# Adding the target rows by an accumulating gather instead of on VectorE, in a graph network's first edge pass

## What is computed

```python
s_n, v_n = _equiv_layernorm(s, v, gamma_s, beta_s, gamma_v)
msg_s = (s_n @ Ws_src)[src] + (s_n @ Ws_dst)[dst]
msg_v = einsum(v_n, Wv_src)[src] + einsum(v_n, Wv_dst)[dst]
w1 = rbf @ W_rbf
m1_s, m1_v = _cg_tp(msg_s, msg_v, y0, y1, w1[...])     # products of msg with the edge's y and w1
a = leaky_relu(m1_s @ W_alpha) . alpha_dot             # logits of a softmax over the edges of a target
val_s, val_v = m1_s @ Ws_val, einsum(m1_v, Wv_val)     # gated, then a second product and h per edge
agg = segment_sum(softmax(a) * h, dst)
```

## Time and profile before

| | before |
|---|---|
| median of 3 runs | 8057.24 us |
| lowest to highest run | 8041.64 to 8085.88 us |
| span of the profiled execution | 8045.0 us |
| VectorE busy, whole span | 7086.7 us, 88% |
| PE busy, whole span | 6926.1 us, 86% |
| POOL busy, whole span | 5439.5 us, 68% |
| the first edge pass | about 312 to 4490 us |
| DMA engines, mean busy share from 400 to 4400 us | 0.40 |

### The profile page before, as it was taken

How to read it: one execution, slowest core, us unless ns; L and a number is a source line. 1 busy time by engine, 2 the same in 40 slices (tenths; PEclk the granted TensorE clock), 3 DMA queues, 4 the chain that set the end, 5 groups by cost and what they waited for, 6 DMA issues and landing times. The chain is left out here.

```text
span 8045.0 us, 198050 instructions
## 1 busy us (share of the span) xinstructions
PE 6926.1 (86%) x44602; PEld 5312.0 (66%) x44603; DVE 7086.7 (88%) x17689; ACT 5126.7 (64%) x15478; POOL 5439.5 (68%) x5263
## 2 busy tenths in 40 slices
PE   7688888888888888888888578889778899999997
PEld 4477777777777777777777477777444445555556
DVE  8599999999999999999999866766677888888887
ACT  3366666666666666666666311116678888999984
POOL 3477777777777777777777276630677777777760
PEclk6699999999999999999999799988899999999999
DMA  6444433333333333333333188884444455555446
GB/s 210 113 104 104 103 104 105 105 104 104 104 105 104 104 104 103 104 105 105 104 104 104 41 255 238 230 174 121 113 124 127 129 131 134 134 134 132 128 121 187
DMA packets 1054709, 1017.38 MB, mean 126 GB/s; under 512 B 460126, under 2 KB 871646, under 8 KB 1054558
## 3 DMA queue, kind: packets, MB, share of 16 engines
q0 software_dynamic: 225792, 385.65, 20.7%
q1 hardware_dynamic: 524080, 354.62, 16.7%
q10 hardware_dynamic: 304784, 276.49, 10.3%
HBM read 685.78 MB, written 330.22 MB: 126 GB/s over the span
## 5 line engine op out<-in xcount | busy, mean ns | idle before, releaser
L717 POOL DMA_INDIRECT e_g_src<-table_src,e_idx x1568 | 1715.3, 1094 | 505.3 <-issue 477.5
L1856 POOL DMA_INDIRECT f_e<-table,f_src x1568 | 1621.0, 1034 | 507.4 <-issue 416.5
L717 POOL DMA_INDIRECT e_g_dst<-table_dst,e_idx x1568 | 1498.2, 955 | 477.8 <-issue 448.5
L1914 PE MATMUL f_ps_a<-f_q,f_onehot 128*128 128x384 f32 x3936 | 1412.1, 502 | 155.7 <-DVE f_q L2004 151.2
L1914 PEld LDWEIGHTS f_ps_a<-f_q,f_onehot 128*128 128x128 f32 x3936 | 712.4, 191 | 679.1 <-DVE f_q L2004 243.2
L841 ACT ACTIVATE e_m1t<-e_ps_t 128x512 f32<-128x512 f32 (+1 forms) x1176 | 657.4, 592 | 303.1 <-PE e_ps_t L754 277.3
L1319 POOL TENSOR_TENSOR r_h<-r_h,logits 128x656 f32<-128x656 f32 x392 | 495.0, 1286 | 384.1 <-DMA r_h<-edge_values 383.4
L754 PE MATMUL e_ps_t<-ident,e_m1v 128*128 128x128 f32 x3136 | 515.6, 287 | 258.4 <-ACT e_m1t L841 129.8
L1379 PE MATMUL r_ps<-r_h,r_onehot 128*128 x3936 | 622.5, 312 | 121.3 <-DVE r_acc L1351 69.7
L1379 PEld LDWEIGHTS r_ps<-r_h,r_onehot 128*128 128x128 f32 x3936 | 565.0, 191 | 178.8 <-issue 175.7
L780 PE MATMUL e_ps_v<-e_w_v,e_m1t 128*128 128x64 f32 x3136 | 649.7, 289 | 0.0
(11 more groups left out here) (269 smaller groups left out, 18015.4 us busy)
## 6 DMA issues: line engine op xcount, KB each, us to landing
edge_values<-e_h ACTq DMA_DIRECT2D x392, 330.0 KB
r_h<-edge_values SPq DMA_DIRECT2D x196, 660.0 KB, 5.8
sums<-f_acc ACTq DMA_DIRECT2D x492, 192.0 KB
sums<-r_acc ACTq DMA_DIRECT2D x492, 82.5 KB, 4.6
e_g_src<-table_src,e_idx POOLq DMA_INDIRECT x1568
e_g_dst<-table_dst,e_idx POOLq DMA_INDIRECT x1568
f_e<-table,f_src POOLq DMA_INDIRECT x1568
f_rbf<-basis SPq DMA_DIRECT2D x492, 48.0 KB
```

Source lines behind the costliest of these rows:

```text
L717: pool.indirect_dma_start(out=into[:, r, t, :], out_offset=None, in_=table, in_offset=bass.IndirectOffsetOnAxis(ap=idx[:, r, c:c + 1], axi ...
L1856: pool.indirect_dma_start(out=rows_of_units[:, place * T + t, :], out_offset=None, in_=table, in_offset=bass.IndirectOffsetOnAxis(ap=src[: ...
L1914: last = nc.tensor.matmul(ps_a[slot][:, 0:ACC1], onehot[:, r, t, :], q[:, r, t, :], start=t == 0, stop=t == T - 1)
```

## The change

The tiles `g_src` and `g_dst` go away. `msg` gets four slots, and both gathers write into it: first the source rows, by a plain indirect DMA, and when these have landed (a new semaphore, `from_src[r]`) the target rows, by an indirect DMA that adds what it brings to what is there (`compute_op=ALU.add`). VectorE's add is left out, and with it one counted step (FIRST 12, DONE_S 7). POOL's loop issues the source rows of group u+3 and then the target rows of group u+2. The source rows of a group wait until all steps of `first_product` of the group four back are done, where before it was its add alone.

```diff
-        g_src = sb("g_src", [P, RING, T, D])
-        g_dst = sb("g_dst", [P, RING, T, D])
-        msg = sb("msg", [P, T, D])
+        msg = sb("msg", [P, RING, T, D])
...
-        FIRST, SECOND, THIRD = 13, 10, 6
-        DONE_S, VREAD, GV = 8, 2, 3
+        FIRST, SECOND, THIRD = 12, 10, 6
+        DONE_S, VREAD, GV = 7, 2, 3
...
-                wait(sp, gathered[r], i * 32 * T)
+                wait(sp, gathered[r], i * 16 * T)
...
+            def rows_of(table, u, r, side, landed, **onto):
+                for t in range(T):
+                    c = side * T + t
+                    pool.indirect_dma_start(
+                        out=msg[:, r, t, :], out_offset=None, in_=table,
+                        in_offset=bass.IndirectOffsetOnAxis(ap=idx[:, r, c:c + 1], axis=0), **onto,
+                    ).then_inc(landed, 16)
+
+            def source_rows(u, r, i):
+                if not present(u):
+                    return
+                pool.wait_ge(idx_in[r], (i + 1) * 16)
+                wait(pool, first, (u - RING + 1) * FIRST if not isinstance(u, int) or u >= RING else 0)
+                pool.sem_inc(issued, 1)
+                rows_of(table_src, u, r, 0, from_src[r])
+
+            def target_rows(u, r, i):
+                if not present(u):
+                    return
+                pool.wait_ge(from_src[r], (i + 1) * 16 * T)
+                pool.sem_inc(issued, 1)
+                rows_of(table_dst, u, r, 1, gathered[r], compute_op=ALU.add)
+
             def body(u, r, i):
-                gather(u + 3, (r + 3) % RING, i + (r + 3) // RING)
+                source_rows(u + 3, (r + 3) % RING, i + (r + 3) // RING)
+                target_rows(u + 2, (r + 2) % RING, i + (r + 2) // RING)
...
-                dve.wait_ge(gathered[r], (i + 1) * 32 * T)
+                dve.wait_ge(gathered[r], (i + 1) * 16 * T)
                 wait(dve, first, u * FIRST)
-                k = d.up(add(msg[:], g_src[:, r], g_dst[:, r]))
                 dve.wait_ge(y_in[r], (i + 1) * 16)
-                dve.wait_ge(first, k)
```

More of the change, by code:

```diff
@@ L614, in edges @@
                                                     sem("ones_set"))
-        idx_in, y_in, rbf_in, gathered = ([sem(f"{n}{r}") for r in range(RING)]
-                                          for n in ("idx_in", "y_in", "rbf_in", "gathered"))
+        idx_in, y_in, rbf_in, from_src, gathered = ([sem(f"{n}{r}") for r in range(RING)]
+                                                    for n in ("idx_in", "y_in", "rbf_in", "from_src", "gathered"))
         stored = [sem(f"stored{r}") for r in range(2)]
@@ L706, in _ @@
             nc.gpsimd.memset(h_rows[:], 1.0).then_inc(ones_set, 1)
-            def gather(u, r, i):
+            def rows_of(table, u, r, side, landed, **onto):
[6 more added lines that the diff above has]
+            def source_rows(u, r, i):
                 if not present(u):
@@ L711, in gather @@
                 pool.wait_ge(idx_in[r], (i + 1) * 16)
-                wait(pool, first, (u - RING) * FIRST + 1 if not isinstance(u, int) or u >= RING else 0)
+                wait(pool, first, (u - RING + 1) * FIRST if not isinstance(u, int) or u >= RING else 0)
                 pool.sem_inc(issued, 1)
[L714 to L720, removed]
-            def body(u, r, i):
-                gather(u + 3, (r + 3) % RING, i + (r + 3) // RING)
-            gather(0, 0, 0)
-            gather(1, 1, 0)
-            gather(2, 2, 0)
+                rows_of(table_src, u, r, 0, from_src[r])
[5 more added lines that the diff above has]
+                rows_of(table_dst, u, r, 1, gathered[r], compute_op=ALU.add)
+            def body(u, r, i):
+                source_rows(u + 3, (r + 3) % RING, i + (r + 3) // RING)
+                target_rows(u + 2, (r + 2) % RING, i + (r + 2) // RING)
+            source_rows(0, 0, 0)
+            source_rows(1, 1, 0)
+            target_rows(0, 0, 0)
+            source_rows(2, 2, 0)
+            target_rows(1, 1, 0)
             rounds(pool, body)
@@ L968, in first_product @@
                 d = Count(first, u, FIRST)
-                s, v = msg[:, :, 0:CS], msg[:, :, CS:D].rearrange("p t (x c) -> p t x c", x=3)
+                s, v = msg[:, r, :, 0:CS], msg[:, r, :, CS:D].rearrange("p t (x c) -> p t x c", x=3)
                 yx = y[:, r, :, 1:4]
```

## The result

The changed kernel takes 8925.67 us (median of 4 runs, 8910.27 to 8941.87) against 8049.44 us for the kernel before on the same chip (8005.45 to 8085.88): **ratio 1.109, 95% interval 1.106 to 1.113**, 876 us slower. The forecast was 8345 us, its range ended at 8850. The direction and the mechanism were right, the size was not.

A forecast was written before the change was run, and what follows sets the result against it. VectorE was taken to bound the edge pass at 10.63 us per group, POOL 0.6 us behind. New period 11.35 us: 0.72 x 392 = 282 us, plus 6 once, onto 8057 gives 8345 us; range 7960 to 8850.

The forecast's parts named there:

- What bounds the kernel: Edge pass: VectorE sets the period of 10.63 us per group; POOL is a second bound 0.6 us behind.
- PE comes third: Edge pass: without its waits for e_h and m1v, PE's chain of a group is about 9.9 us.
- equal price: Rival: POOL is charged nothing for accumulation; period about 10.5 us, 8012 us; equal or nearly equal price had chance 0.44.
- The hold-up of a gather: POOL's gathers wait on VectorE operations with two SBUF inputs: 0.14 to 0.84 us per group without the add.
- The price of an accumulating gather: On POOL, each target gather that adds costs +0.2 us over a plain one, 0.8 us per group; bounds 0 and 0.95.
- The rule set against that term: Skill's rule that many descriptors can be emitted before incremental cost shows: accumulation term zero, period about 10.5 us.
- The new wait: POOL's wait for landed source rows before each target group: already satisfied, cost nothing unless landings grew over 10 us.
- the longer wait for `first`: POOL waits for all of first_product of the group four back, not only its add: already satisfied.
- The DMA engines: Four target gathers take 1.4 us; if accumulating doubles them, the engines' share goes from 0.40 to about 0.53: hidden.
- VectorE's idle time: VectorE idles before a group's first vy until target rows land; busy share falls from 99% to about 86%.

## Why the prediction was right or wrong

- **What bounds the kernel: right.** VectorE first, POOL 0.6 us behind it. Without the add the period is 10.48 and 10.50 us, in the forecast's 10.14 to 10.84 and at its middle, 10.5; the times of 8001 and 7984 us stand beside the 8012 of "equal price". That PE comes third, at 9.9 us, no run tests: none came below 10.48. The hold-up of a gather by VectorE's operations with two SBUF inputs, read from the earlier trace rows, gave that number; the Trainium skill's rule (SBUF — State Buffer, Who interferes with whom) and these runs agree.
- **The price of an accumulating gather: the step that failed.** The term was +0.2 us, measured is +0.61. The other terms hold: 4 x 1.25 + 4 x 1.86 + 0.4 = 12.8 us. The bounds were right, 0 to 0.95, but the value was argued from a fixed part that does not grow, and the runs show the opposite: the fixed part is what grows, by some 0.45 us, and the rows' part by about 0.15. With 0.61 in the forecast's own sum, 4 x 1.25 + 4 x 1.86 + 0.55 = 12.99, 2.36 x 392 + 6 = 931 and 8988 us, 0.7% above what was measured.
- **The range** stopped at +0.5 us per gather (8850), though the text kept 0.95 as the upper bound. A tenth was given to all beyond it; for a cost that no row showed that was too little, and the range should have gone to the bound, 4 x 0.45 = 1.8 us more per group.
- **The rule set against that term** (the Trainium skill, DMA: Bandwidth & Descriptors, Anatomy of one DMA: many descriptors before the cost shows) fits what rows and bytes did on POOL: 96 rows fewer save 0.09 us of a plain gather and 0.20 of one that adds, and half the bytes nothing. It says nothing of the fixed price of an accumulating DMA, and as a rival it lost: 0.61 us, not zero.
- **The new wait: right.** 0.3 us in 311 groups. So is the longer wait for `first` (1.8 us in all), and the changed order: with no tile accumulated the ratio is 1.000.
- **The DMA engines: right.** Queue 0 had 25.9% of the engines, 2.75 us of a group. After:

```profile
q0 software_dynamic: 179337, 153.15, 31.5%
```

  31.5% of 12.90 is 4.06 us, so, if the source gathers kept theirs, the four target gathers went from 1.4 to 2.7 us, the doubling that was allowed for, and hidden.
- **VectorE's idle time: right in kind, sized by the same term.** It falls to 76% busy, where 86% was forecast.
- **Unforeseen:** that the sign of the change depends on the condition of the chip. The prediction took the granted clock of 1.00 in the earlier trace rows as given.

## What to carry to other kernels

An engine whose busy share is 77% may have no slack at all: look at the gaps between its instructions, and at what the next engine's period is, before its load is raised to relieve another. A gather that adds costs POOL two thirds more than one that doesn't, most of it per instruction and not per row or byte, so if a DMA has to add, let it be one large one (1.01 us for four tiles). Before a last per cent is taken out of the busiest engine, take the whole operation away and time that; here it would have said about 1%. And since the ranking was reversed under the other condition of the chip, kernels are compared with the kernel before of the same session only.

## What the runs showed of the hardware

- POOL's time for an indirect DMA of 128 rows of 640 bytes: 0.95 us plain, 1.54 to 1.59 accumulating; for 64 rows 0.90 and 1.41 to 1.48; for 32 rows 0.86 and 1.34 to 1.40; for 128 rows of 320 bytes 0.94 and 1.54 to 1.59. A direct accumulating DMA of 128 x 640 numbers from SBUF to SBUF: 1.01, and never over 1.04 beside VectorE's work, where the plain indirect ones reach 1.42.
- Where before had a granted clock of 1.00 in the pass, which is 2.4 GHz, kernels with more pauses on PE had a lower mean: 0.98 at a period of 11.29 us, 0.95 at 11.77, 0.90 at 12.83. Each of these is a mean over the stretch, between that level and the lower one of 1.2 GHz. Under the other condition the mean goes neither by the period nor by POOL's pace: 0.77 at 16.9, 0.69 at 16.9, 0.72 at 15.7, 0.86 at 13.1 and 13.2.
- Two engines can run at one period though no wait of one for the other is longer than an ordinary gap (0.3 us): POOL's eight gathers would take 10.0 us alone and take VectorE's 10.62 on average over the whole pass, by hold-ups of 0.63 us. That these settle at just that value because POOL runs ahead until they do is the prediction's reading; no run tests it.
